# A mask added by VectorE during the maximum search, in place of a mask product on TensorE

## The reference, cut to what matters

```python
q = _split_heads(query @ Wq.T + bq)
k = _split_heads(key @ Wk.T + bk)
v = _split_heads(value @ Wv.T + bv)
scores = jnp.einsum('bhqd,bhkd->bhqk', q, k) / np.sqrt(D_K)
scores = jnp.where(mask[:, None, :, :] == 0, jnp.float32(-1000000000.0), scores)
p_attn = jax.nn.softmax(scores, axis=-1)
attn = jnp.einsum('bhqk,bhkd->bhqd', p_attn, v)
```

## Time and profile before

| | before |
|---|---|
| median of 3 runs | 1255.24 us (1255.02 to 1257.88) |
| profiled execution | 1258.71 us |
| its span, first to last instruction | 1256.9 us |
| TensorE busy | 982.3 us (78%) |
| VectorE busy | 753.0 us (60%) |
| ScalarE busy | 626.6 us (50%) |
| GpSimd busy | 582.6 us (46%) |

### The profile page before, as it was taken

The page is one execution under the profiler, slowest core; times in us unless marked ns, Lnnn a source line. Parts: engine busy times, 40 slices in busy tenths (PEclk is TensorE's granted clock), DMA queues, the critical chain, the costliest instruction groups (busy, mean ns, idle before and its releaser), DMA issues.

```text
span 1256.9 us, 17423 instructions
## 1 busy us (share of the span) xinstructions
PE 982.3 (78%) x5204; PEld 702.5 (56%) x5204; DVE 753.0 (60%) x1764; ACT 626.6 (50%) x1875; POOL 582.6 (46%) x637
## 2 busy tenths in 40 slices
PE   6440899990686997888889798888988888887772
PEld 6220688880454665565566566556656656654551
DVE  3525476662374685787578577657857867654232
ACT  2531466650242765655555565655555655644440
POOL 2477433332546247446444653634555354531213
PEclk9965799995798999989988998998899999967565
DMA  9799587646101001021102102100210200200000
GB/s 281 236 357 343 178 285 252 239 179 87 22 1 27 8 5 35 7 30 24 22 6 33 34 8 36 26 14 10 30 37 5 36 10 7 36 5 11 7 4 5
DMA packets 126513, 93.66 MB, mean 75 GB/s; under 512 B 77546, under 2 KB 105684, under 8 KB 121684
## 3 DMA queue, kind: packets, MB, share of 16 engines
q1 hardware_dynamic: 121268, 82.05, 24.4%
q0 software_dynamic: 4096, 8.40, 2.5%
q10 hardware_dynamic: 1056, 2.10, 0.6%
HBM read 59.46 MB, written 33.06 MB: 74 GB/s over the span
## 4 chain that ended last, share of the span: by engine, by line
PE 45%; POOL 22%; DVE 12%; issue 10%; ACT 9%; DMA 2%; SPq 0%; POOLq 0%; DVEq 0%; ACTq 0%
ACT pr L764 6%; PE U L1119 5%; POOL xs_dram L511 5%; POOL yg L563 5%; PE M L1316 5%; PE U L1123 4%; PE U L1120 4%; PE M L1322 4%; POOL h_lo L572 4%; PE M L1349 3%; DVE xin L962 3%; PE Y L1123 2%; PE M L1313 2%; PE M L1361 2%; PE Y L1119 2%
## 5 line engine op out<-in xcount | busy, mean ns | idle before, releaser
L572 POOL TENSOR_TENSOR h_lo<-h,h_hi 128x512 fp32r<-128x512 f32 x128 | 164.9, 1289 | 240.4 <-ACT h_hi L735 240.0
L764 ACT ACTIVATE pr<-M,nmax 128x128 f32<-128x128 f32 x512 | 180.7, 370 | 51.2 <-DVE nmax L1058 50.9
L729 ACT ACTIVATE h<-U 128x512 f32<-128x512 f32 x128 | 76.4, 597 | 147.1 <-PE U L1123 146.8
L1058 DVE TENSOR_REDUCE nmax<-M 128x4 f32<-128x512 f32 x128 | 87.4, 683 | 87.3 <-PE M L1316 86.7
L1119 PE MATMUL U<-xn_hi,w_hi 128*128 128x512 f32 x256 | 126.0, 492 | 8.2 <-DVE h L1007 6.4
L1003 DVE SCALAR_TENSOR_TENSOR h<-h,U 128x512 f32<-128x512 f32 x128 | 87.6, 684 | 74.6 <-ACT h L729 74.4
L1322 PE MATMUL M<-ident,pr 128*128 128x128 f32 x512 | 87.4, 298 | 54.5 <-ACT pr L764 54.4
L1123 PE MATMUL U<-xn_lo,w_hi 128*128 128x512 f32 x256 | 108.9, 426 | 0.0
L1120 PE MATMUL U<-xn_hi,w_lo 128*128 128x512 f32 x256 | 108.6, 424 | 0.0
L1322 PEld LDWEIGHTS M<-ident,pr 128*128 128x128 f32 x512 | 62.7, 151 | 81.8 <-issue 62.7
L764 ACT ACTIVATION_READ_ACCUMULATOR pr<-M,nmax 128x1 f32 x512 | 107.4, 210 | 0.0
(11 more groups left out here) (307 smaller groups left out, 2328.8 us busy)
## 6 DMA issues: line engine op xcount, KB each, us to landing
wt<-w_dram SPq DMA_DIRECT2D x23, 1024.0 KB, 4.8
w_dram<-wt SPq DMA_DIRECT2D x8, 1024.0 KB, 8.6
xs_dram<-xr SPq DMA_DIRECT2D x1, 5888.0 KB, 20.7
ys_dram<-acc SPq DMA_DIRECT2D x12, 256.0 KB, 2.3
key_stack<-k_dram SPq DMA_DIRECT2D x48, 64.0 KB
wt<-k_dram SPq DMA_DIRECT2D x48, 64.0 KB
ys_dram<-part SPq DMA_DIRECT2D x11, 256.0 KB, 2.3
pr<-in_L_xattn_W SPq DMA_DIRECT2D x8, 256.0 KB, 6.6
```

What stands on the lines that cost most here:

```text
L572: nc.gpsimd.tensor_tensor(h_lo[i % 4][:, :], h32[i % 3][:, :], h_hi[i % 4][:, :].bitcast(fp32), ALU.subtract).then_inc(lo_done, 1)
L764: done = nc.scalar.activation(pr[i % 2][:, c], bank[:, c], ACT.Exp, bias=nmax[i % 4][:, r:r + 1], accum_out=rsum[b % 2][:, HB * r + j:HB * ...
L1058: nc.vector.tensor_reduce(nmax[i % 4][:, :], m_bank(("s", i))[0][:, :].rearrange("p (h k) -> p h k", h=HB), AX.X, ALU.max, negate=True).th ...
```

## The change

The unit-matrix product is gone and the four score products each open their own sum. The mask is now +2^100 where the mask is 0 and is kept in plain fp32. Query weights and bias are scaled with -1/sqrt(8), so that PSUM holds negated scores. VectorE runs four operations per step, one for each head: it adds the mask to 128x128 of PSUM, writes the sum back to the same place, and gives the minimum, which is the negated maximum of the masked scores, to `nmax`. The exponential is taken with a scale of -1. VectorE's mask waits for VectorE's own searches instead of TensorE's scores, the first search of a row waits for the mask, and TensorE no longer does. The orders of the engines are as before.

```diff
-MASKED = -2.0 ** 100
+MASKED = 2.0 ** 100
...
-        mneg = [sb(f"mneg{i}", [P, S], fp32r) for i in range(2)]
+        mneg = [sb(f"mneg{i}", [P, S]) for i in range(2)]
...
-                                 ACT.Copy, scale=DK ** -0.5)
+                                 ACT.Copy, scale=-DK ** -0.5)
...
-            for w, dst, scale in ((0, WqT, DK ** -0.5), (1, WkT, 1.0)):
+            for w, dst, scale in ((0, WqT, -DK ** -0.5), (1, WkT, 1.0)):
...
-                        done = nc.scalar.activation(pr[i % 2][:, c], bank[:, c], ACT.Exp, bias=nmax[i % 4][:, r:r + 1], accum_out=rsum[b % 2][:, HB * r + j:HB * r + j + 1])
+                        done = nc.scalar.activation(pr[i % 2][:, c], bank[:, c], ACT.Exp, bias=nmax[i % 4][:, r:r + 1], scale=-1.0, accum_out=rsum[b % 2][:, HB * r + j:HB * r + j + 1])
...
-                        dve.wait_ge(m_full, m_at["s", (i - 1) * HB - 1] + 1)
+                        dve.wait_ge(nmax_done, (i - 1) * HB)
...
-                    nc.vector.tensor_reduce(nmax[i % 4][:, :], m_bank(("s", i))[0][:, :].rearrange("p (h k) -> p h k", h=HB), AX.X, ALU.max, negate=True).then_inc(nmax_done, 1)
+                    if i % HB == 0:
+                        dve.wait_ge(mask_made, i // HB + 1)
+                    bank = m_bank(("s", i))[0]
+                    for r in range(HB):
+                        c = slice(r * S, (r + 1) * S)
+                        ins = nc.vector.tensor_tensor_reduce(bank[:, c], bank[:, c], mneg[i // HB % 2][:, :], 1.0, BIG, ALU.add, ALU.min, nmax[i % 4][:, r:r + 1])
+                    ins.then_inc(nmax_done, 1)
...
-                        pe.wait_ge(mask_made, b + 1)
...
-                    nc.tensor.matmul(bank[:, :], ident_r[:, :], mneg[b % 2][:, :].unsqueeze(1).broadcast_to([P, HB, S]), start=True, stop=False)
...
-                        ins = nc.tensor.matmul(bank[:, h * S:(h + 1) * S], qst[g % 2][rows, h, t], kst[g % 2][rows, h, t], start=False, stop=(h == HB - 1))
+                        ins = nc.tensor.matmul(bank[:, h * S:(h + 1) * S], qst[g % 2][rows, h, t], kst[g % 2][rows, h, t], start=True, stop=True)
```

## The result

| | before | after |
|---|---|---|
| first measurement, same chip: median | 1258.99 us | 1246.05 us |
| ratio, 95% interval | | 0.9896 (0.9872 to 0.992) |
| second measurement, another chip: median | 1257.84 us | 1248.86 us |
| ratio, 95% interval | | 0.9922 (0.9895 to 0.9949) |
| span of the first profiled execution | 1256.9 us | 1243.5 us |

The kernel became faster: by 13 us in the first measurement and by about 10 in the second. The forecast was 6.4 us less, at 1248.8 us; the sign and the range held, and the gain is larger than the sum said. That 1248.8 lies so close to the measured 1246.05 is in part luck: the three runs that the forecast started from have a median of 1255.24 us, and sixteen runs of the same kernel gave 1258.99.

A forecast was written before the change was run, and what follows sets the result against it. The prediction took the order of waits, not a full engine, as the bound. A 12.3 us debit less an 18.7 us credit gave -6.4 us, from 1255.2 to 1248.8 us; own range 1240 to 1253, overall 1237 to 1275.

The forecast's parts named there:

- the sum: Whole kernel: 12.3 us for the longer search less 18.7 us for the removed mask products, -6.4 us, median 1248.8 us.
- What bounds the kernel: Attention steps, 406 to 1219 us: no engine is full, so the order of waits between engines decides.
- The quick step: Step at 410.63 us: exponentials wait behind the expert layer's tanh, search has 0.70 us to spare; turn 4.53 to some 4.3.
- the late one: Step at 863.91 us: exponentials wait for VectorE's search, so a longer search costs its whole length, half a microsecond.
- The credit: 128 mask products leave TensorE; 82 pieces on the chain of waits, 24.9 us, three quarters credited: 18.7 us.
- The length of the search: VectorE, each attention step: four operations for one take 1.17 us, 0.49 longer; bounds 0.19 and 1.09 longer.
- The debit: Attention steps: the longer search beyond spare time costs 17.5 us, less 5.2 covered by GpSimd, so 12.3 us.
- counting of spare times: All 128 steps: the search's lengthening less ScalarE's and TensorE's spare time, summed; 25 steps have under 0.1 us.
- The terms put at nothing: Exponentials' scale of -1, set-up scalings, scores opening own sums, VectorE's mask and its waits, TensorE's dropped wait: no cost or gain.
- The slow search: Steps with little spare time: at 0.82 us longer, 13.8 us slower, 1269; sums cross at about 0.60; chance 0.31.
- Free read-outs: VectorE's search only 0.19 us longer: 15.1 us faster, 1240, or 1234 with the whole credit; chance 0.10.
- that rival: 406 to 1111 us: less TensorE work lowers the granted clock to 0.92, costing 6.3 us, 1255; chance 0.19 with other waits.

The follow-up runs named there:

- e1: The changed kernel with a useless TensorE product of the mask product's size put back ahead of the scores; 1266.98 us, 1.0077 of before.
- e2: The kernel before without its mask product, scores unmasked, search still one instruction; 0.9872 and 0.9873 of before in two measurements.
- e7: The changed kernel with a useless TensorE product put ahead of the transposes' wait for the exponentials; 1248.97 us, 0.9901 of before.
- e4: The changed kernel with the search writing masked scores to SBUF, where the exponentials work in place; 1247.79 us, 0.9892 of before.
- e3: The changed kernel with two wide VectorE operations, mask addition then minimum over four heads, in place of the four; 1268.95 us, 1.0094 of before.
- e9: The kernel before without its mask product, scores unmasked, plus a useless product ahead of the transposes' wait; 1242.02 us, 0.9867 of before.
- e5: The changed kernel with the search writing to SBUF and each head handed to ScalarE as soon as searched; 1245.77 us, 0.9899 of before.
- e8: The kernel of e5 with a useless TensorE product ahead of the transposes' wait; 0.9857 of before, second time 0.9908.

## Why the prediction came out as it did

**What bounds the kernel.** Right in both kinds of step, as far as the steps shown go. The quick step turned in 4.29 us (forecast some 4.3) and the late one grew by 0.41 us, the search's lengthening. e1 and e2 show the two terms in the waits: the tanh's wait for TensorE follows the product, the exponentials' wait for VectorE follows the search.

**The credit**, three quarters of the chain's 24.9 us, 18.7: measured 16 without the longer search and 19 to 23 with it. The choice held as a number, but its reason, that another arrival takes over, is not shown: by the price of the clock that the executions suggest, the missing quarter of e2 could as well be the clock's. So that the number held is in part luck. e7 shows that a piece on the chain is no cost in itself: in a quick step the product is on it and the turn is no longer.

**The length of the search** was taken as 0.49 us more and is 0.42. The read-out costs 140 ns as an instruction but lies beside the next pass, so the four cost three distances of 0.21 to 0.25 us and one pass with its read-out (0.39 us), not four of 0.275. The Trainium skill's estimate, from the page VectorE: DVE Perf Modes, section on the TRN2 errata, was 0.258 us for each instruction and 0.375 more in all; the trace's 0.25 us between passes agrees with it. The Trainium skill gives this figure for what goes from PSUM to SBUF, though, and there the trace differs: in e4, whose search writes to SBUF, a pass starts 0.21 us after the one before (412.43 and 412.64). By that estimate of the Trainium skill the prediction had worked out a gain of some 10 us, nearer than its own 6.4. What the Trainium skill says on the same page in "Two Vector instructions with no wait between them", that an output of the accumulator is an instruction of its own, is now in the rows: L1063 is two groups.

**The debit** is the step that was mis-sized. It stood at 12.3 us; with the measured 0.42 us the same counting of spare times gives 9.8, and e1 measured 9.7 (5.4 to 13.8) beside the product. What was off in it is the read-out, counted as 0.075 us more in each of the four, where it lies beside the next pass. Put into the sum, 9.8 - 18.7 = -8.9, within the second measurement's interval and 1 us outside the first. Without the product the debit looks smaller still: from e2's 0.987 to the kernel after it is 3 to 6 us. That would mean that the two terms share steps, and that less TensorE work leaves searches more time, or that the lower clock of e2 hides part of the debit; but 9.7 against 3 to 6 is a difference of four ratios that each carry some 0.3%, so it stays open whether the terms add. The terms put at nothing are all in e1, and the exponentials take 369 ns after and 370 before; nothing there shows a cost.

**The rivals.** The slow search is real, but not at this length: with 0.74 us more the kernel is 11.8 us slower than before (e3), and the crossing that the prediction put at 0.60 us comes out at 0.58 on a straight line. Free read-outs didn't come: the search is 0.42 us longer and not 0.19, so that the first measurement's 13 us lie near that case's 15.1 without its cause. The clock fell, as that rival said, to 0.93 and in the second profile to 0.92, which the prediction had named as a sign of being wrong. The sign did not tell, since the kernel after is faster at 0.92 too. But the rival is not refuted as a part of the sum: raising the clock with a product (e7, e9) brought no net gain, product and clock together, and what the clock alone is worth is not separated. The estimate from the executions is some 5 us taken back.

**The other signs.** The four operations were to span 1.1 to 1.3 us: 1.10. More than 36 exponentials were to wait for the search: 58. VectorE's share of the chain was to stay near 12% plus 12 us, some 13%: it is 17%, and this sign was wrong. The chain follows one of several nearly equal ways; e7 moves 4% of it from VectorE to TensorE and leaves the time where it was. TensorE's own share fell from 45% to 42%, so the mask's 2% went to no other line of TensorE, as forecast.

**The two misses, e4 and e5**, had the same root: each costed the side that was looked at (longer exponentials, an earlier hand-over) and left out what the edit does to the other engine. For e4 the other side was measured. For e5 it was not found: the waits that it shortens are in the profile, and what takes their place is open. Its executions have a mean clock of 0.850 against 0.860 after, which by the price above would be some 7 us, an estimate.

## What to carry to other kernels

Work that is moved from a busy engine to an emptier one is judged step by step: in steps where the next engine waits for something else the move is free, in those where the receiving engine is late it costs its whole length, and the length at which the two balance (here 0.6 us per step) could be read from the spare times before anything was built. A line's share of the chain of waits was a bound here for what its removal gave, and two thirds to nine tenths of it came back; a share that rises afterwards is no sign of a loss. The clock of each execution is worth listing beside its time: it can say more about the clock's price than a second kernel in which something else changes too. Before an operation is split or fused, look at the distance between starts in a row of such instructions and not at the durations: four pairs of a pass (320 ns) and a read-out (140 ns) took 1.10 us, two wide operations of 692 ns, the second waiting for the first, took 1.43.

## What had not been expected of the hardware

VectorE's pass and its read-out are shorter when the pass writes to SBUF than when it writes back in place to PSUM: 285 and 83 ns against 320 and 140. ScalarE's exponential goes the other way by its source, 369 ns from PSUM and 391 from SBUF, where it works in place. The Trainium skill, page ScalarE: Activation LUTs (Step-by-step: what each stage is for), says that ScalarE stands closer to PSUM and VectorE closer to SBUF; it says so of where results go, and VectorE's rows agree.

A TensorE product that nobody reads, put where TensorE waits, raised the granted clock from 0.93 to 0.95 (e7) and from 0.91 to 0.94 (e8 against e5) and cost no net time that could be measured. In the quick step shown the product is free; whether it is free in the others too or the higher clock pays for it there is open. The 58 executions of the kernel before, 6.7 us apart for 0.01 of the clock, speak for the second.
